# Layer 2's rows stay on chip, the turned weights load during the final chain, and the token sums swap operands

## The reference, cut to what matters

```python
x = x + gnn(xn, edges) + mix(xn)          # gnn: two graph layers; mix: linear attention
y = layernorm(x)
w = softmax(((y @ W_x + b_x) @ W_slice + b_slice) / temp)  # by head: 8 heads of 64 slots, over the slots
s = w.T @ (y @ W_fx + b_fx) / (sum(w) + 1e-5)             # tokens, by head
p = attention(s @ W_q, s @ W_k, s @ W_v)                  # among the 64 tokens of a head
out = x + (w @ p) @ W_out + b_out
```

## Time and profile before

| what | us |
|---|---|
| median of 3 runs | 2003.83 (2000.82 to 2005.24) |
| the profiled execution | 2000.85 |
| its span, first to last instruction | 1999.0 |

### The profile page before, as it was taken

The page is one execution under the profiler, slowest core; times in us unless marked ns, Lnnn a source line. Parts: engine busy times, 40 slices in busy tenths (PEclk is TensorE's granted clock), DMA queues, the critical chain, the costliest instruction groups (busy, mean ns, idle before and its releaser), DMA issues. The chain is left out here.

```text
span 1999.0 us, 45233 instructions
## 1 busy us (share of the span) xinstructions
PE 1879.2 (94%) x18843; PEld 1409.5 (71%) x18843; DVE 1182.2 (59%) x2699; ACT 851.9 (43%) x1970; POOL 299.6 (15%) x417
## 2 busy tenths in 40 slices
PE   3599989999999999999979999999999999999598
PEld 3255555555555555555569999999999999998477
DVE  6899987666666666666515555555555555555322
ACT  1577765566566656666512222222222222222100
POOL 3143110000000000000020111111111111111033
PEclk7699989999999999999989999999999999999799
DMA  3133322323222232222344444444444444442087
GB/s 98 56 114 108 96 82 98 130 98 126 102 106 122 98 130 98 117 111 98 130 160 140 145 146 146 146 145 146 145 146 145 142 143 144 145 138 81 13 273 242
DMA packets 92701, 252.13 MB, mean 126 GB/s; under 512 B 14142, under 2 KB 59346, under 8 KB 79938
## 3 DMA queue, kind: packets, MB, share of 16 engines
q1 hardware_dynamic: 69225, 218.83, 30.8%
q10 hardware_dynamic: 21096, 25.65, 3.6%
q0 software_dynamic: 2176, 4.75, 0.9%
HBM read 131.99 MB, written 118.02 MB: 125 GB/s over the span
## 5 line engine op out<-in xcount | busy, mean ns | idle before, releaser
L1390 PE MATMUL ps<-hs,at 128*128 128x512 f16 x2401 | 667.1, 378 | 0.4 <-POOL at L1207 0.3
L1609 PE MATMUL ps<-at,big 128*128 128x128 f16 x9604 | 577.3, 219 | 6.5 <-DMA at<-at_scratch 6.5
L1609 PEld LDWEIGHTS ps<-at,big 128*128 128x128 f16 x9604 | 556.3, 98 | 34.3 <-issue 8.1
L1446 ACT CAST at<-ps 128x392 f16<-128x392 f32 x784 | 375.7, 487 | 286.7 <-PE ps L1351 271.3
L1351 PE MATMUL ps<-big 128*128 128x98 f16 x3136 | 470.8, 208 | 7.3 <-DVE big L1291 7.1
L1351 PEld LDWEIGHTS ps<-big 128*128 128x128 f16 x3136 | 297.0, 97 | 141.0 <-DVE big L1291 8.9
L1390 PEld LDWEIGHTS ps<-hs,at 128*128 128x128 f16 x2401 | 229.6, 97 | 148.2 <-issue 0.5
L1291 DVE TENSOR_TENSOR big<-iota_lo,key_lo 128x1024 f16<-128x1024 f16 x392 | 268.7, 685 | 0.0
L1291 DVE TENSOR_TENSOR big<-iota_hi,key_hi 128x784 f16<-128x784 f16 x392 | 219.3, 559 | 0.0
L1723 DVE SCALAR_TENSOR_TENSOR big<-ps,small,blogb 128x512 f32<-128x512 f32 x49 | 36.8, 751 | 230.6 <-PE ps L1645 230.6
L1826 POOL TENSOR_TENSOR key_lo<-key_lo,big 128x512 f32<-128x512 f32 (+1 forms) x49 | 61.9, 1264 | 706.6 <-ACT big L1784 706.6
(11 more groups left out here) (280 smaller groups left out, 2285.3 us busy)
## 6 DMA issues: line engine op xcount, KB each, us to landing
at_scratch<-at SPq DMA_DIRECT2D x49, 1568.0 KB, 5.2
at<-at_scratch SPq DMA_DIRECT2D x49, 1568.0 KB, 6.9
xT_scratch<-big SPq DMA_DIRECT2D x98, 128.0 KB, 1.8
big<-xT_scratch SPq DMA_DIRECT2D x49, 256.0 KB, 3.2
wT_scratch<-big ACTq DMA_DIRECT2D x49, 256.0 KB, 2.0
hs<-wT_scratch SPq DMA_DIRECT2D x49, 256.0 KB, 3.5
big<-in_x_dram SPq DMA_DIRECT2D x96, 128.0 KB, 2.3
x_scratch<-big ACTq DMA_DIRECT2D x48, 128.0 KB, 1.7
```

What stands on the lines that cost most here:

```text
L1390: mm = te.matmul(ps[:, 2 + b, :], lhsT=at[:, b, k * P:(k + 1) * P], rhs=hs[:, k, :], start=(k == 0), stop=(k == T - 1))
L1446: a.copy(to.rearrange("p k (i j) -> p k i j", j=WIN), ps[:, BANKS[m % len(BANKS)], 0:UW * KC].rearrange("p (i k j) -> p k i j", i=UW, j=WI ...
L1609: mm = te.matmul(ps[:, b, c * NT:(c + 1) * NT], lhsT=hs2[:, k, h * C + c * P:h * C + (c + 1) * P], rhs=at[:, b, k * P:(k + 1) * P], start= ...
```

## The change

- x1 of all 49 tiles stays on chip, in the memory of layer 1's features (`hs`), which layer 2 does not read. The store to DRAM goes, and so do the loads in the stream. The constants of the final chain move to the end of the upper half of `big`.
- POOL adds the last bias (`bfb`) to x1 in layer 2, behind the wait for `xn2_ready`, which says that DVE has read x1.
- The token sums are made with the normed row as the stationary operand (a block of 128 columns) and all 512 slots of the weights as the moving one: two blocks times three pairs, 6 products. The sums then stand in PSUM as the chain's first product wants them; DVE copies one bank and ACT the other, and the turns at the chain's start go.
- The stream moves into the chain's block. SP loads the turned weights of the first 36 tiles into memory that is free by then (`hs2`, 24 tiles, and `at`, 12), from the start of the chain, four transfers in flight; a later tile waits until its slot is multiplied.
- The last product of the chain signals twice; DVE copies the first half of `pmat`, ACT the second.
- Two of POOL's zero fills move from the start of layer 2 to the start of the chain.

```diff
-            x1 = take([P, 2, C])
+        x1 = hs_f32.rearrange("p (t c) -> p t c", c=C)
...
-                    for p in range(HB):
-                        for w_half, x_half in ((ewh, xn2h), (ewh, xn2l), (ewl, xn2h)):
-                            mm = te.matmul(ps[:, 6 + p // 2, (p % 2) * C:(p % 2 + 1) * C],
-                                           lhsT=w_half[0:rows(t), b, p * P:(p + 1) * P], rhs=x_half[0:rows(t), b, :],
-                                           start=False, stop=False, skip_group_check=True)
+                    for c in range(CB):
+                        for w_half, x_half in ((ewh, xn2h), (ewl, xn2h), (ewh, xn2l)):
+                            mm = te.matmul(ps[:, 6 + c, :], lhsT=x_half[0:rows(t), b, c * P:(c + 1) * P],
+                                           rhs=w_half[0:rows(t), b, :], start=False, stop=False, skip_group_check=True)
...
-                v.tensor_scalar(s_sum.rearrange("p a b -> p (a b)"), ps[:, 6:8, :].rearrange("p a b -> p (a b)"),
-                                1.0 / WS, None, ALU.mult)
+                v.tensor_scalar(sT[:, 0].rearrange("p a b -> p (a b)"), ps[:, 6, :], 1.0 / WS, None, ALU.mult)
...
-                    act.dma_start(x1_dram[bass.ds(t * NT, rows(t)), :], x1[0:rows(t), b, :]).then_inc(x1_out[b], 16)
...
+                act.wait_ge(s_added, T)
+                a.mul(sT[:, 1].rearrange("p a b -> p (a b)"), ps[:, 7, :], 1.0 / WS)
...
+                        pool.wait_ge(xn2_ready, t + 1)
+                        g.tensor_tensor(x1[0:NT, t, :], x1[0:NT, t, :], bfb, ALU.add)
                         pool.wait_ge(wt_ready, t + 1)
...
+            @block.sync
+            def _(sp):
+                for t in range(T):
+                    if t >= SLOTS:
+                        sp.wait_ge(mixed, t - SLOTS + 1)
+                    if t >= IN_SEMS:
+                        sp.wait_ge(w_in[t % IN_SEMS], 16 * (t // IN_SEMS))
+                    sp.dma_start(turned_rows[t % SLOTS], wT_dram[bass.ds(t, 1)].rearrange("t p n -> (t p) n")
+                                 ).then_inc(w_in[t % IN_SEMS], 16)
...
-                for i in range(CB):
-                    for p in range(HB):
-                        mm = te.transpose(ps[:, i, p * P:(p + 1) * P], s_sum[:, p, i * P:(i + 1) * P], ident[:, :])
-                mm.then_inc(pe_step, 1)
-                pe.wait_ge(act_step, 1)
...
-                mm.then_inc(pe_step, 1)
+                    if p % 2 == 1:
+                        mm.then_inc(pe_step, 1)
+                pe.wait_ge(pmat_ready, 2)
+                for t in range(T):
+                    pe.wait_ge(w_in[t % IN_SEMS], 16 * (t // IN_SEMS + 1))
+                    if t >= 4:
+                        pe.wait_ge(summed, t - 3)
+                    for p in range(HB):
+                        mm = te.matmul(ps[0:rows(t), 4 + t % 4, 0:C], lhsT=turned_rows[t % SLOTS][:, p * NT:p * NT + rows(t)],
+                                       rhs=pmat[:, p, :], start=(p == 0), stop=(p == HB - 1))
+                    mm.then_inc(mixed, 1)
...
+                act.wait_ge(pe_step, 8)
+                a.copy(pmat[:, 2:4].rearrange("p a b -> p (a b)"), ps[:, 3, :]).then_inc(pmat_ready, 1)
+                for t in range(T):
+                    act.wait_ge(summed, t + 1)
+                    act.dma_start(out[bass.ds(t * NT, rows(t)), :], x1[0:rows(t), t, :]).then_inc(rows_out, 16)
...
-                dve.wait_ge(pe_step, 8)
-                v.tensor_copy(pmat.rearrange("p a b -> p (a b)"), ps[:, 2:4, :].rearrange("p a b -> p (a b)"))
+                dve.wait_ge(pe_step, 7)
+                v.tensor_copy(pmat[:, 0:2].rearrange("p a b -> p (a b)"), ps[:, 2, :]).then_inc(pmat_ready, 1)
+                for t in range(T):
+                    dve.wait_ge(mixed, t + 1)
+                    v.tensor_tensor(x1[0:rows(t), t, :], ps[0:rows(t), 4 + t % 4, 0:C], x1[0:rows(t), t, :],
+                                    ALU.add).then_inc(summed, 1)
```

More of the change, by code:

```diff
@@ L923, in _ @@
                 pipeline(tile, T, RING, lead=2, lag=3)
[L930 to L987, removed]
-                        nc.vector.tensor_tensor(res[0:rows(t), b, :], ps[0:rows(t), b, 0:C], rows_in[0:rows(t), b, :],
-                                                ALU.add).then_inc(s_ready, 1)
-                    pipeline(tile, T, NB)
-                @block.scalar
-                def _(act):
-                    def tile(t, b, u):
-                        act.wait_ge(s_ready, t + 1 + past)
-                        act.dma_start(to[bass.ds(t * NT, rows(t)), :], res[0:rows(t), b, :]).then_inc(s_out[b], 16)
-                    pipeline(tile, T, NB)
-                    for b in range(NB):
-                        act.wait_ge(s_out[b], 16 * (len(range(b, T, NB)) + past_in(b)))
@@ L1512, in gps_layer @@
         take = carve(key_lo[:, :].bitcast(F32))
-        s_sum = take([P, HB, C])
+        sT = take([P, CB, HB, P])
         w_sum = take([P, HB])
@@ L1530, in gps_layer @@
         bdv = take([P, P])
-        sT = take([P, CB, HB, P])
+        bfb = take([P, C])
+        take = carve(late_f[:, 0:T * C - FINAL_WORDS])
+        pmat = take([P, HB, C])
         tok = take([P, HB, P])
@@ L1543, in gps_layer @@
         wrec = take([P, HB])
-        tmp = take([P, D])
         zeroed, loaded = sem("f_zeroed"), sem("f_loaded")
@@ L1547, in gps_layer @@
         with ExitStack() as stage:
-            take = carve(big_f[:, T * C:])
+            take = carve(late_f[:, 0:T * C - FINAL_WORDS])
             aggT = take([P, 2, CB, NT])
@@ L1834, in gps_layer, with _ @@
             pe_step, dve_step, act_step = sem("f_pe_step"), sem("f_dve_step"), sem("f_act_step")
-            block = stage.enter_context(nc.Block())
+            early = hs2.rearrange("p t c -> p (t c)").bitcast(F32)
+            SLOTS_1, SLOTS_2 = T * C // (HB * NT), T * P // (HB * NT)
+            SLOTS = SLOTS_1 + SLOTS_2
+            turned_rows = [(early if s < SLOTS_1 else at_f32)[:, n * HB * NT:(n + 1) * HB * NT]
+                           for s in range(SLOTS) for n in (s if s < SLOTS_1 else s - SLOTS_1,)]
+            IN_SEMS = 4
+            w_in = [sem(f"w_in{r}") for r in range(IN_SEMS)]
+            mixed, summed = sem("f_mixed"), sem("f_summed")
+            rows_out, cleared, pmat_ready = sem("rows_out"), sem("f_cleared"), sem("pmat_ready")
+            block = stage.enter_context(nc.Block())
+            @block.sync
[7 more added lines that the diff above has]
+                                 ).then_inc(w_in[t % IN_SEMS], 16)
+            @block.gpsimd
+            def _(pool):
+                g = nc.gpsimd
+                for z in (tok, at_w):
+                    last = g.memset(z, 0.0)
+                last.then_inc(cleared, 1)
             @block.tensor
@@ L1948, in _ @@
                 last.then_inc(dve_step, 1)
-                dve.wait_ge(pe_step, 8)
-                v.tensor_copy(pmat.rearrange("p a b -> p (a b)"), ps[:, 2:4, :].rearrange("p a b -> p (a b)"))
-        stream(0, final_rest, lambda t: wT_dram[bass.ds(t, 1)].rearrange("t p n -> (t p) n"), x1_dram,
-               [pmat[:, p, :] for p in range(HB)], bfb, out)
+                dve.wait_ge(pe_step, 7)
[4 more added lines that the diff above has]
+                                    ALU.add).then_inc(summed, 1)
 _INS = ['x', 'src', 'dst', 'L0_gnn_W1', 'L0_gnn_b1', 'L0_gnn_W2', 'L0_gnn_b2', 'L0_mix_W_qkv', 'L0_mix_b_qkv',
```

51 lines of the change are left out of this document (22 added, 29 removed).

## The result

The changed kernel takes 1990.99 us (median of 3 runs, 1990.71 to 1991.08) against 2003.83 (2000.82 to 2005.24): the ratio is 0.9935, 95% interval 0.9919 to 0.9951, the difference 12.8 us. The forecast was 1991.5 (1985.5 to 1998). In a second set of runs on one chip the same kernel took 1993.42 against 2004.70, ratio 0.9935 (0.9922 to 0.9947), a difference of 11.3 us where the sum of the terms was 11.6.

What follows compares the result with a forecast made beforehand. TensorE bounds layer 2's body; gains lie at the seams and in the stream's waits. Terms -0.5 + 0.4 - 2.7 - 3.8 - 5.0 = -11.6 us give 1989.3 from the profiled run, 1992.2 from the median; forecast 1991.5, range 1985.5 to 1998.

Steps and rivals of the forecast that it cites:

- Token sums: Layer 2: six products of 512 columns replace twelve of 256, -0.5 us on 48 tiles, between -2 and +1.
- Bias in layer 2, hidden in the body: Layer 2's body: POOL's added addition delays VectorE 0.4 to 1.05 us a tile, hidden by its 1.64 us wait: 0.
- Drain +0.4: Layer 2's last tile: POOL's addition meets VectorE's cast with nothing to hide it, +0.4 us, between 0 and 1.05.
- Layer 2 to chain, -2.7: Last token sum to the chain's first product: 3.70 us falls to 0.99, -2.7 us; gain between 2.2 and 3.0.
- Chain to stream, -3.8: Chain's last product to the stream's first: 4.50 us falls to 0.68, -3.8 us, or -3.2 if ACT's copy doubles.
- Weights in time: Chain and stream: turned weights load at 0.9 us a tile, used at 1.725; late only at 2.3 us a tile.
- One sign I named: Chain: all 36 early loads of turned weights would be done before the stream.
- Stream, -5.0: Stream of 92.05 us: waits for x1's loads go with x1 on chip, -5.0 us, between -3.8 and -7.2.
- the far end of this term: Stream's start: half-clock loss of 3.4 us if the clock rises later by as much as half.
- Clock of the stream's start: Stream's start: half clock persists as before, mean 0.63 over 5.94 us, the same 2.2 us lost.
- The first rival: Stream starts at full clock because no long gap is left: 2.2 us more gain, 1989.5 us, chance 0.14.

Runs made afterwards that it cites:

- sums as before: Changed kernel with only the swapped operands undone, so twelve token sums of 256 columns and the turns return: 1996.68 us, ratio 0.9952 to the kernel before.
- five POOL additions: Changed kernel with four more POOL additions of 128x256 per tile of layer 2, into spare memory: 1993.27 us, ratio 0.9941 to the kernel before.
- bias late: Changed kernel with POOL adding the last bias to the last two tiles at the chain's start, not in layer 2: 1992.93 us, one run.
- all kept busy: Changed kernel with unread products in TensorE's waits of layer 2's last two tiles and the chain, last two tiles' bias at the chain's start: 1981.07 us, ratio 0.9874.
- no wait for the store: Against "all kept busy", SP instead of ACT at layer 2's end awaits the last two stores of turned weights: 1981.46 us, ratio 0.9885 to the kernel before.

## Why the prediction was right, step by step

- **Token sums.** -0.5 forecast for the body. The time from tile to tile went from 16.920 to 16.905 us (mean of 41), which is -0.7 on 48 tiles; with the sums as before it was 16.920 again.
- **Bias in layer 2, hidden in the body.** Shown: VectorE's wait shrank by 0.42 us, and PE waits for nothing in the body even with five additions. What bears the cost is the second split, not the cast, from which I took the price: the cast took 0.83 us before already. (The Trainium skill's page SBUF — State Buffer, section Who interferes with whom, lets the engine that issues first hold the shared ports for its whole instruction, while the other blocks. The trace agrees on who meets whom. When the split began, 0.55 us of POOL's 0.91 were left (1814.79 to 1815.34), and the split grew by 0.40: most of what was left, and well under the 1.05 that I set as the far end.)
- **Drain +0.4.** Shown by the last tile's cast: 0.43 before, 0.83 now and 0.43 with the bias late.
- **Layer 2 to chain, -2.7.** 1.00 us against 0.99 forecast. The turns and ACT's copy are 3.3 of it when they are put back alone, at the lower clock. The last store of wT was ahead of the copy's end, as I had it: it was issued at 1865.35 and landed 2.0 us later, at 1867.36, 0.6 ahead (0.3 in my sum). When the drain got shorter, the store and POOL both fell behind the copy.
- **Chain to stream, -3.8.** 0.68 us as forecast, released by ACT's copy. 2.1 of it hang on the early loads.
- **Weights in time.** 0.88 us a tile against 0.9 forecast and 1.725 used; no wait for them. One sign I named could not come true by my own sum: 36 loads at 0.9 us are 32 us and the chain is 28, so the last of the 36 were issued in the stream. The trace has them so.
- **Stream, -5.0.** -4.83. The additions are 1.726 us apart up to the last. The attribution needs a correction: the waits for x1's loads went, but with x1 still coming from DRAM and the weights loaded ahead there were none either. The prediction credited x1's place for what either part buys. The waits stood where 147 transfers went through a ring of 4 at a DMA share of 0.92; how much of them is the ring and how much the share is not shown. At the far end of this term the loss should read 3.3, not 3.4: half as much again as 4.4 us at half clock, half of it lost.
- **Clock of the stream's start.** 0.62 over the first 6 us, as the forecast took it (0.63). The first rival's 2.2 us are real: 84.91 us wherever the clock was full at the start. Its reason is not: with the gap down to 0.68 us the start stayed at 0.62. Among the eight profiles of changed kernels in which nothing fills the chain's waits a full clock came once, after the chain of "five POOL additions", so the chance of 0.14 was not far off; what decided it there is not shown. (The Trainium skill's page TensorE: Matmul & The Clock Gate, section HAM oscillation — how this bites in real kernels, has idle gaps send the clock back. Filling the gaps of the chain gave 0.93 there and 1.00 in the stream, which agrees.)
- **What I did not count.** The unchanged part ahead of layer 2 moves by some 5 us from one execution to the next. It is nearly half of the gain, and single spans compared whole would have told a wrong size: -9.8. So it is luck that the forecast lies within 0.5 us of the median: the same kernel gave 1993.42 in the second set, with single runs from 1986.20 to 1993.98. The stages are not luck of that kind, each within 0.3 us of its term.

## What to carry to other kernels

Price a change stage by stage, in the stage whose wait ends last, and compare single profiles from a point where their code starts to differ. When two parts of a change remove the same wait, or two waits end together, undo them one at a time and both at once: one alone tells either "everything" or "nothing". Look at the clock of a serial chain of small products: here filling its waits with products that nothing reads gave 7.9 us (5.6 and 2.3) on top of the 11.7 of the change.

## What the hardware showed that I had not expected

- A chain of dependent products ran at the lower clock for most of its length (mean 0.68 of full, which is 0.64 of the time at half), and the stream behind it began at 0.62 over 6.12 us; 93 products that nothing reads took 5.6 us off the one and 2.3 off the other.
- The change of block took 0.30 us for VectorE when VectorE was last, but the next block began 1.31 us behind the end of POOL's last addition in "five POOL additions", "all kept busy" and "no wait for the store". In the last of these POOL ended 0.16 us before VectorE and still set the change of block: with its addition gone the step fell from 1.88 to 1.00 us.
- Where POOL's addition and VectorE's second split met, the one that started second paid: the split 0.40 us (0.69 to 1.09) behind the addition to x1, and in "five POOL additions" POOL, whose first of four additions began during the split and took 1.06 us, while the three behind it took 2.43 together.
- Loads at a DMA share of 0.86 and 274 GB/s beside the chain cost it nothing that shows: 28.36 us without, 28.32 with, at a mean clock of 0.68 in both.
